# Second cross attention: keys of two chunks projected in one visit of the tensor array

## The reference

```python
q = (x @ Wq).reshape(b, n, H, DH)                 # H = 16, DH = 64, n = 1024
k = (context @ Wk * SCALE).reshape(b, m, H, DH)   # m = 6404
v = (context @ Wv).reshape(b, m, H, DH)
scores = jnp.einsum('bihd,bjhd->bhij', q, k)
attn = jax.nn.softmax(scores, axis=-1)
out = jnp.einsum('bhij,bjhd->bihd', attn, v)
return out.reshape(b, n, H * DH) @ Wo + bo
```

## Time and profile before

| | |
|---|---|
| median of 3 runs | 4777.79 us (4776.16 to 4780.69) |
| profiled execution | 4784.57 us, its span 4782.5 us |
| granted TensorE clock, mean of the span | 0.926 |
| TensorE, busy share of the span | 91% |
| TensorE weight loads | 45% |
| VectorE | 59% |
| ScalarE | 51% |
| GpSimd | 59% |
| the stage's heads | about 2390 to 4640 us of the span |

### The profile page before, as it was taken

How to read it: one execution, slowest core, us unless ns; L and a number is a source line. 1 busy time by engine, 2 the same in 40 slices (tenths; PEclk the granted TensorE clock), 3 DMA queues, 4 the chain that set the end, 5 groups by cost and what they waited for, 6 DMA issues and landing times. The chain is left out here.

```text
span 4782.5 us, 68907 instructions
## 1 busy us (share of the span) xinstructions
PE 4329.2 (91%) x21823; PEld 2153.7 (45%) x21823; DVE 2806.1 (59%) x3447; ACT 2436.3 (51%) x4388; POOL 2820.9 (59%) x1598
## 2 busy tenths in 40 slices
PE   6988879989898998799699999999999999999973
PEld 2333345545454555233445445454444545445431
DVE  3656576868686685556655555555555555555405
ACT  1344555657565564155355555555555555555530
POOL 0000075758576573000198888888888897888880
PEclk8678889999999999588799999999999999999985
DMA  0000000000000000000100000000000000000000
GB/s 19 3 3 0 0 37 23 3 25 12 14 15 12 19 6 4 9 1 1 33 2 2 3 3 1 4 1 3 3 3 2 1 4 2 3 3 1 1 0 10
DMA packets 17985, 34.62 MB, mean 7 GB/s; under 512 B 3418, under 2 KB 12250, under 8 KB 16746
## 3 DMA queue, kind: packets, MB, share of 16 engines
q1 hardware_dynamic: 17642, 30.22, 2.0%
HBM read 29.69 MB, written 0.52 MB: 6 GB/s over the span
## 5 line engine op out<-in xcount | busy, mean ns | idle before, releaser
L1190 POOL TENSOR_TENSOR xat_p_sum<-xat_p_sum,xat_p_full 128x1024 f32<-128x1024 f32 x768 | 1833.6, 2387 | 230.4 <-ACT xat_p_full L1140 194.4
L1231 DVE TENSOR_REDUCE xat_part<-xat_ring 128x2 f32<-128x1024 f32 (+1 forms) x815 | 934.0, 1182 | 549.9 <-PE xat_ring L1009 547.1
L1140 ACT ACTIVATE xat_p_full<-xat_sc 128x512 f32<-128x512 f32 (+1 forms) x1632 | 870.1, 593 | 727.4 <-PE xat_sc L1049 691.4
L1035 PE MATMUL xat_acc<-xat_p_full,xat_v 128*64 128x512 f32 (+1 forms) x3264 | 792.0, 605 | 0.0
L1048 PE MATMUL xat_sc<-xat_q_hh,xat_k_hl 128*128 128x512 f32 (+1 forms) x1632 | 777.3, 476 | 15.1 <-ACT xat_p_full L1140 13.7
L1049 PE MATMUL xat_sc<-xat_q_lm,xat_k_h 128*128 128x512 f32 (+1 forms) x1632 | 645.7, 396 | 0.0
L1048 PEld LDWEIGHTS xat_sc<-xat_q_hh,xat_k_hl 128*128 128x128 f32 (+1 forms) x1632 | 303.5, 186 | 302.1 <-issue 155.6
L1882 POOL TENSOR_TENSOR loc_weights_n<-loc_probs,loc_rinv 128x512 f32<-128x512 f32 (+1 forms) x384 | 326.1, 870 | 169.4 <-DVE loc_rinv L2012 169.3
L1866 POOL TENSOR_TENSOR loc_sind<-loc_qk,loc_tab 128x512 f32<-128x512 f32 x192 | 239.8, 1272 | 229.9 <-DVE loc_squares L1935 168.6
L1035 PEld LDWEIGHTS xat_acc<-xat_p_full,xat_v 128*64 128x64 f32 (+1 forms) x3264 | 197.0, 136 | 368.7 <-issue 290.0
L1532 PE MATMUL loc_pr<-loc_w_qkv,loc_xs 128*128 128x512 f32 x576 | 296.8, 640 | 55.9 <-DVE loc_cosd L1929 42.9
(11 more groups left out here) (418 smaller groups left out, 6851.4 us busy)
## 6 DMA issues: line engine op xcount, KB each, us to landing
loc_w_qkv<-in_L_ffn_w SPq DMA_DIRECT2D x6, 1536.0 KB, 7.4
loc_w_o<-in_L_ffn_wo SPq DMA_DIRECT2D x6, 512.0 KB, 3.5
xat_ctxT<-in_ctxT SPq DMA_DIRECT2D x12, 256.0 KB, 2.7
xat_w_qk<-in_L_xattn_wqk SPq DMA_DIRECT2D x16, 128.0 KB, 2.0
loc_w<-in_L_ffn_w SPq DMA_DIRECT2D x6, 341.0 KB, 3.0
loc_w<-in_L_ffn_w SPq DMA_DIRECT2D x6, 192.0 KB, 2.3
loc_rope<-in_rope SPq DMA_DIRECT2D x1, 1024.0 KB
xat_w_o<-in_L_xattn_wo SPq DMA_DIRECT2D x16, 64.0 KB, 1.8
```

Source lines behind the costliest of these rows:

```text
L1035: last = pe.matmul(acc[h * GROUP:(h + 1) * GROUP, :], v[0:size, t, e * GROUP:(e + 1) * GROUP], p_full[0:size, (e * NT + t) % RING, cols(h) ...
L1140: act.activation(p_full[0:size, at_.buffer(t), cols(h)], sc[0:size, n % 3, :], ACT.Exp, scale=GROUP ** -0.5).then_inc(S["exp_done"], 1)
L1190: pool.tensor_tensor(p_sum[:, e, :], first_in, p_full[:, at_.buffer(t), :], ALU.add)\
L1231: ins = dve.tensor_reduce(part[:, 2 * t:2 * t + 2, c], slot[:, :, 0:chunks[c][1]], AX.X, ALU.max)
```

## The change

Two chunks of keys are projected into one ring slot, as two products of 64 weight columns. The one for the lower chunk writes the partitions 0 to 63 of the slot's first bank, the other the partitions 64 to 127 of its second. The pairs are (11, 12) at step 0, and (0, 1), (2, 3), (4, 5), (6, 7), (8, 9) at the steps 4, 8, 12, 16, 20; chunk 10 stays alone at step 22, in the old form. Of each chunk one half of the partitions holds the product, and ScalarE copies it to both places: the first chunk's two copies stand ahead of the exponentials of the step's second tile, the second chunk's two behind them. VectorE subtracts twice, once for each chunk, and the slot is given back by the second subtraction. The copies into `k_h1` move to the next step, behind its exponentials. The number of M per step is now a table (`MAXIMA`); the ring has 74 items in an odd head where it had 80, and 66 where it had 72 in an even one. The weights, the arithmetic and the first pass are as before.

```diff
+    SIDE = {0: (OWN, 2), **{2 * c + 4: (c, 2) for c in range(0, OWN - 1, 2)}, 2 * OWN: (OWN - 1, 1)}
+    KEYS_IN = lambda c, count: [(h, c + h, *chunks[c + h]) for h in range(count)]
+    MAXIMA = (0, 2, 2, 2, 1, 2, 1, 2, 2, 2, 3, 3, 2, 2, 3, 2, 2, 2, 3, 2, 2, 3, 2, 3, 2)
...
-                for n, c in enumerate(order):
-                    steps[n if c >= OWN else 2 * c + 2][pre] += [("K", c, 0)]
+                for j, (c, count) in SIDE.items():
+                    steps[j][pre] += [("K", c, count)]
                 maxima = [("M", c, m) for c in order for m in range(NTOK // 2)]
                 for j in range(1, NJ - 1):
-                    here = {4: 1, 6: 1}.get(j, 2) if j <= 6 else -(-len(maxima) // (NJ - 1 - j))
-                    for k in range(here):
+                    for k in range(MAXIMA[j]):
                         steps[j][mid if j == 4 or k >= 2 else post] += [maxima.pop(0)]
...
                     elif kind == "K":
-                        lo, width = chunks[c]
                         if part is first:
                             pe.wait_ge(S["ctx_loaded"], 16 * (order.index(c) + 1))
-                        last = pe.matmul(slot[:, 0, 0:width], w_qk[:, nxt, P:2 * P], ctxT[:, lo:lo + width],
-                                         start=True, stop=True)
+                        if t == 2:
+                            for h, _, lo, width in reversed(KEYS_IN(c, t)):
+                                half = slice(h * GROUP, (h + 1) * GROUP)
+                                last = pe.matmul(slot[half, h, 0:width], w_qk[:, nxt, P + h * GROUP:P + (h + 1) * GROUP],
+                                                 ctxT[:, lo:lo + width], start=True, stop=True)
+                        else:
+                            lo, width = chunks[c]
+                            last = pe.matmul(slot[:, 0, 0:width], w_qk[:, nxt, P:2 * P], ctxT[:, lo:lo + width],
+                                             start=True, stop=True)
...
                     elif kind == "K":
-                        hi += 1
-                        lo, width = chunks[c]
-                        lo = key_at(nxt, lo)
-                        act.activation(k_up[GROUP:P, order.index(c) % 3, 0:width], slot[GROUP:P, 0, 0:width],
-                                       ACT.Copy)
-                        act.activation(k_hl[0:GROUP, lo:lo + width], slot[0:GROUP, 0, 0:width], ACT.Copy)\
-                           .then_inc(S["hi_done"], 1)
-                        copies.append((lo, width, hi))
+                        for h, cc, lo, width in KEYS_IN(c, t):
+                            if h:
+                                for late in pairs[j][1:]:
+                                    weights(late)
+                            hi += 1
+                            lo = key_at(nxt, lo)
+                            upper = slot[GROUP * h:GROUP * h + GROUP, h, :] if t == 2 else slot[GROUP:P, 0, :]
+                            lower = upper if t == 2 else slot[0:GROUP, 0, :]
+                            act.activation(k_up[GROUP:P, order.index(cc) % 3, 0:width], upper[:, 0:width], ACT.Copy)
+                            act.activation(k_hl[0:GROUP, lo:lo + width], lower[:, 0:width], ACT.Copy)\
+                               .then_inc(S["hi_done"], 1)
+                            copies.append((lo, width, hi))
...
+                copies = []
                 for j, (pre, _, _) in enumerate(part.steps):
-                    copies = []
+                    due = len(copies)
...
-                    if part.sums:
+                    if part.sums and not (part.fills and SIDE.get(j, (0, 0))[1] == 2):
                         for t in pairs[j][1:]:
                             weights(t)
...
-                    for lo, width, n in copies:
+                    due = due if part.sums else len(copies)
+                    for lo, width, n in copies[:due]:
                         act.wait_ge(S["hi_done"], at_.heads(NCH + 1, NCH + 1 + n))
                         act.activation(k_h1[0:GROUP, lo:lo + width], k_hl[0:GROUP, lo:lo + width], ACT.Copy)\
                            .then_inc(S["copy_done"], 1)
+                    copies = copies[due:]
...
                         elif kind == "K":
-                            lo, width = chunks[c]
-                            key = slice(key_at(nxt, lo), key_at(nxt, lo) + width)
-                            ins = dve.tensor_tensor(k_hl[GROUP:P, key], slot[GROUP:P, 0, 0:width],
-                                                    k_up[GROUP:P, order.index(c) % 3, 0:width], ALU.subtract)
+                            for h, cc, lo, width in KEYS_IN(c, t):
+                                hi += 1
+                                dve.wait_ge(S["hi_done"], at_.heads(NCH + 1, NCH + 1 + hi))
+                                key = slice(key_at(nxt, lo), key_at(nxt, lo) + width)
+                                if t == 2 and h == 0:
+                                    product, high = slot[0:GROUP, h, 0:width], k_hl[0:GROUP, key]
+                                else:
+                                    product = slot[GROUP:P, h, 0:width]
+                                    high = k_up[GROUP:P, order.index(cc) % 3, 0:width]
+                                ins = dve.tensor_tensor(k_hl[GROUP:P, key], product, high, ALU.subtract)
```

More of the change, by code:

```diff
@@ L796, in __init__ @@
                 where = {item: (j, k) for j, step in enumerate(steps) for k, items in enumerate(step) for item in items}
+                filled = {c + h: where["K", c, count] for c, count in SIDE.values() for h in range(count)}
                 for n, c in enumerate(order):
-                    assert where["K", c, 0] < where["M", c, 0]
-                    assert n + 3 >= NCH or where["M", c, NTOK // 2 - 1] < where["K", order[n + 3], 0]
+                    assert all(filled[c] < where["M", c, m] for m in range(NTOK // 2))
+                    assert n + 3 >= NCH or where["M", c, NTOK // 2 - 1] < filled[order[n + 3]]
             elif fills:
@@ L802, in __init__ @@
                 for n, c in enumerate(order):
-                    steps[n + 1][pre] += [("K", c, 0)]
+                    steps[n + 1][pre] += [("K", c, 1)]
                     steps[n + 2][mid] += [("M", c, m) for m in range(NTOK // 2)]
@@ L1163, in body @@
                            .then_inc(S["copy_done"], 1)
+                    copies = copies[due:]
+                assert not copies
             run(act, body)
@@ L1215, in body @@
                         slot = place_of(at_, l)
-                        if kind in "QK":
+                        if kind == "Q":
                             hi += 1
                             dve.wait_ge(S["hi_done"], at_.heads(NCH + 1, NCH + 1 + hi))
-                        else:
+                        elif kind != "K":
                             dve.wait_ge(S["ring_ps"], at_.shown(l + 1))
```

## The result

| | before | changed |
|---|---|---|
| median, runs measured together | 4779.24 us (4776.16 to 4784.1, 4 runs) | 4855.98 us (4839.29 to 4868.2, 4 runs) |
| ratio | | 1.0154, 95% interval 1.0133 to 1.0176 |
| profiled execution, its span | 4784.57, 4782.5 | 4839.29, 4837.3 |
| the stage, first query projection to last weighting | 2332.16 | 2406.34 |
| an odd head, an even head | 145.2, 139.5 | 150.0, 144.2 |

The account below looks back on a forecast made before the run. TensorE's own order was taken to bound the second cross attention. Per head -2.60 + 6.88 + 0.34 - 1.12 = +3.50 us, over 15 heads less 1.4 is +51: 4829 us, range 4775 to 4872.

Parts of the forecast that it names:

- rival (a): Whole kernel: slower as summed, TensorE waiting for the ring slot; 4829 us, chance 0.74.
- the sum: All terms per head: -2.60 + 6.88 + 0.34 - 1.12 = +3.50 us; over 15 heads, less 1.4, +51 us.
- Part 1: Key projection on TensorE: a pair costs 1.20 us instead of 2 x 0.86; five pairs save 2.60 a head.
- sign: TensorE over the whole run: busy time some 35 us lower while the span is longer.
- Rival (d): Pair on TensorE: halves do not run side by side, 1.72 + 0.34 a pair; 77 us more, 4906; chance 0.06.
- Part 2: Ring slot held longer: TensorE waits, 1.37 us in steps 8, 12, 16, 20 and 1.40 in step 4; +6.88 a head.
- The softmax sum: Step 4, the slot's next user: would come at +5.33 and wait to +6.73, 1.40 us.
- The crossing of partitions: ScalarE's copies and VectorE's subtraction: same durations assumed; a fifth slower would lengthen the chain 0.5, about +35 us.
- Part 3: Steps 0 and 1, both tail chunks in step 0: ScalarE's chain to an awaited exponential grows, net +0.34 us a head.
- Part 4: Maxima items: three waits for VectorE in steps 8, 10 and 12 go, -1.12 us a head.
- (b): Ring slot free before TensorE asks, so no new wait: -3.38 us a head, 4727 us; chance 0.12.
- Rival (c): Wait for the ring slot half as long: 3.4 us a head less, 4778, within 0.2%; chance 0.08.

Follow-up runs that it names:

- e4_full_width: Changed kernel with each pair's two products at the full 128 columns, one behind the other: 4938.02 us, ratio 1.0329 to before.
- e7_full_width_one_behind: Changed kernel with the edit of e4_full_width and the maxima table of e2_one_behind together: 4804.05 us, ratio 1.0059 to before.
- e3_table_alone: Kernel before with only its maxima formula replaced by the change's table, keys still in single chunks: 4791.6 us, ratio 1.0006.
- e2_one_behind: Changed kernel with another MAXIMA table: one M instead of two behind the weighting in steps 8, 12, 16, 20, none in step 4: 4762.51 us, ratio 0.9952.
- e1_both_ahead: Changed kernel with ScalarE making both chunks' copies ahead of the second tile's exponentials: 4790.54 us, ratio 1.001 to before.

## Why the prediction was right, and where its sum fell short

The forecast was 4829 by rival (a); 4855.98 came, slower by the mechanism that it named, with 77 us instead of 51. An odd head was to take about 150 instead of 146.8, and takes 150.0; that fit is luck. The head of the earlier trace rows had 1.6 us of lower clock at its start, so at full clock it is 145.2 and 150.0, a growth of 4.8 where the sum has 3.5. Step by step:

**Part 1, the pair: right.** From low product to low product, with the pair between them, it is 1.67 (3194.24 to 3195.91), where 1.66 was forecast from the earlier trace rows. Those rows are of products over 4 partitions and not 128, so the form was not quite the same; it made no difference. Steps that lost their keys are 0.82 to 0.84 shorter where nothing else changed (steps 2 and 6). TensorE's busy time fell by 48.6 us, where some 35 were given as a sign. Rival (d) is what e4_full_width and e7_full_width_one_behind were made to be, and both are slower than their partners with the halves side by side.

**Part 2, the hold of the slot: right in kind, 0.2 a wait too small.** TensorE asks at +5.46 in the sum; the step's first M at +5.14 and an unbroken pair's 0.33 make +5.47. The slot was to be seen free at +6.73 and was at +6.96. The links:

| link | predicted | measured |
|---|---|---|
| pair to first copy | 1.07 | 1.13 |
| first to second copy | 0.60 | 0.60 |
| copy to exponentials | 0.50 | 0.50 |
| exponentials to the second chunk's first copy | 0.95 | 1.08 |
| copy to copy | 0.60 | 0.61 |
| copy to subtraction | 0.63 | 0.63 |
| subtraction, to TensorE | 0.69 + 0.10 | 0.69 + 0.13 |

The links add up to 0.23 more than forecast, and the mis-sized one is the fourth, 0.13; the first adds 0.06, the last 0.03. The sum took 0.95 from the earlier trace rows, because the `k_h1` copy stands in that place; but the operation that comes there now is a copy out of the ring, and the earlier trace rows had exactly that behind exponentials: 3100.82 to 3101.91, 1.09. The `k_h1` copy starts 0.1 before the exponentials end, the ring's copy after. The row of the same operation was at hand, and the row of the same place was taken. In step 16 the wait costs 1.59 instead of 1.37: 3198.11 to 3199.93 less the 0.33 of an unbroken pair is 1.49, and the 0.43 to the next score holds 0.10 more. The other three keys steps are 7.32 and not 7.39 long, 0.07 less. So the four are some 0.7 a head above the sum. The softmax sum adds 0.2: step 4 grew by 1.94 for a forecast of 0.34 + 1.40.

**The crossing of partitions costs nothing.** The first chunk's subtraction reads the partitions 0 to 63 and writes 64 to 127: 0.68, against 0.69 of the one that stays where it is. Copies take 0.59 either way. (When they may start is another matter, below.)

**Part 3, steps 0 and 1: +0.60, predicted +0.34.** TensorE waits as foretold, released by ScalarE:

```profile
3107.57 0.40 PE L1058 MATMUL xat_sc<-xat_q_lm,xat_k_h 128*128 128x512 f32 x1
3108.86 0.51 PE L1057 MATMUL xat_sc<-xat_q_hh,xat_k_hl 128*128 128x512 f32 x1 [0.90 <-ACT xat_p_full L1153]
```

ScalarE's chain to that exponential (between the copies of step 0 and the exponentials of 3108.22):

```profile
3105.84 1.06 ACT L1153 ACTIVATE xat_p_full<-xat_sc 128x512 f32<-128x512 f32 x2
3106.92 0.38 ACT L1125 ACTIVATE xat_k_up<-xat_ring 64x260 fp32r<-64x260 f32 x1
3107.32 0.39 ACT L1126 ACTIVATE xat_k_hl<-xat_ring 64x260 fp32r<-64x260 f32 x1
3107.73 0.60 ACT L1173 ACTIVATE xat_o_raw<-xat_acc 128x512 f32<-128x512 f32 x1
3108.22 2.06 ACT L1153 ACTIVATE xat_p_full<-xat_sc 128x512 f32<-128x512 f32 x4
```

Here too exponentials to the ring's copy is 1.08, where the accumulator's copy followed at 0.95: 0.13 of the difference. The small copies follow each other at 0.40 and 0.41 instead of 0.38 (0.05), and the first copy comes 0.16 later behind the score ahead of the projection (3103.30 to 3104.74, before 3096.48 to 3097.76), where the sum had 0.10. That leaves 0.02.

**Part 4, the maxima: right.** Steps 10 and 12 have no wait of that kind any more; step 10 is 1.24 shorter, 0.86 of it the keys and 0.38 the wait (predicted 0.42). That the table alone gains nothing (e3_table_alone) agrees: without the pair the waits only move to steps 14 and 18.

**The sum.** 3.50 + 0.70 + 0.20 + 0.26 = 4.66 a head; another 0.1 is in steps 2, 6 and 10, which gave back 0.02 to 0.04 less each than the sum had. The table of steps has 4.80, an even head some 4.7. Fifteen heads, less 1.4 for the first, are some 70, where 51 were forecast; the stage grew by 74.2, the rest of it by clock, and what is left up to the medians' 77 is within the runs' scatter. The upper end of the range, 4872, came from copies a fifth slower; it held for another reason than the one given.

**Rivals (b) and (c).** The slot was not free in time, so (b) fell; but e2_one_behind shows that the same hold gives a gain if TensorE comes later, with 104 us in the stage between the two, against the 102 between (a) and (b). Rival (c), a wait half as long and no change to speak of, was nearly what e1_both_ahead made: 0.36 instead of 1.33, and no measurable change. With the changed kernel's own order it did not come.

## What to carry to other kernels

When two pieces of work share a buffer, sum the whole chain of readers up to its release, and find who asks for the buffer next: the cheap remedy may be to move that user one item later, not to shorten the hold. Take each link from a row of the same operation, not from whatever stands in that place now. Packing pays where the pieces are full-sized; a small piece may cost more through its readers than it saves on the array (0.10 us here, against a wait of 0.90).

## What was not expected of the hardware

- **The clock after a wait.** In e4_full_width, waits of 1.43 to 1.52 us in even heads were mostly followed by a fall of the granted clock (in the stretches shown 0.64 and then 0.83), and each fall cost some 1.5 us; waits of 1.24 to 1.37 for the slot in the changed kernel never were. Of the seven odd heads of e4_full_width, with waits of the same lengths, only the first had one such fall, and the even head 14 had none. So the length of the wait alone does not decide it. What makes the difference stays open: no run varied that alone.
- **ScalarE's starts.** An exponential starts about 0.1 us before the copy ahead of it has ended (3196.29 + 0.59 against 3196.79), and so does the copy to `k_h1` behind exponentials. A copy into `k_up` never does (3196.79 + 1.06 against 3197.87). Nor does what stands behind a second chunk's copy into `k_hl`, which reads partitions 64 to 127: in e1_both_ahead the exponential behind it starts 0.03 after its end (3201.35 + 0.59 against 3201.97). In all nine profiles the keys' copies keep to this: behind a copy that reads or writes the upper half of the partitions the next operation starts 0.01 us or more after its end, behind one that stays in the lower half 0.1 before it, unless the next is a copy into `k_up`. `k_h1` and `k_up` are written in the same type and from 64 partitions each, so neither of these decides it. The half of the partitions fits every row, but no run varied it alone.
- **The time ahead of the stage.** In nine profiles the stage starts between 2283.9 and 2316.0 us, with the same work ahead of it, and the changed kernel's stage repeats to 1.1 us (2406.3 and 2405.2). A profile's span is compared by stages, or it says little below 30 us.
